# Two attentions and an expert layer on one core: the prologue's projections over several PSUM banks, its transfers and rows in another order, and the second batch's causal attention split around the first batch's eight-wide queries

## The chip, the cores and the metric

The kernel runs on one NeuronCore of a Trainium2 chip. The metric is the device time of one execution in microseconds (us); lower is better. A core has TensorE (PE, matrix multiplies into PSUM), VectorE (DVE), ScalarE (ACT), GpSimd (POOL) and SyncE (SP, which here only issues transfers). Each engine runs its own instruction list in order; they meet at semaphores. PSUM has eight banks, and each is named in this kernel: scores0 to scores2, max0 to max2, out and side.

## The reference, cut to what matters

There are eight batches of 512 tokens by 256 features. Each goes through a modulated layer norm, a causal attention with 16 heads of width 16, a gate and a residual; then a second modulated layer norm, a third norm with an affine, an attention without mask with 32 heads of width 8 (here called the eight-wide attention), and experts with a gelu.

```
mod = (_silu(L0_c) @ L0_wmod).reshape(L0_c.shape[0], 6, 1, -1)
h = _layernorm(x, axis=-1) * (1 + ca) + sa
x = x + ga * _L0_attn_ref(h, q_proj, k_proj, v_proj, o_proj)       # 16 heads of width 16, causal
h = _layernorm(x, axis=-1) * (1 + cb) + sb
    xn = (x - mu) / jnp.sqrt(var + 1e-05) * ln_g + ln_b
    att = jnp.einsum('bqhd,bkhd->bhqk', q, k) / np.float32(np.sqrt(hd))   # 32 heads of width 8
    o = jnp.einsum('bhqk,bkhd->bqhd', p, v).reshape(B, S, D) @ wo + x
    h = jax.nn.gelu(jnp.einsum('metd,edf->metf', xe, w1) + b1[None, :, None, :], approximate=False)
    y = jnp.einsum('metf,efd->metd', h, w2) + b2[None, :, None, :]
x = x + gb * _L0_ffn_ref(h, ...)
```

## The kernel before

**Pieces.** The work is a list of items, such as `("scores", off, a, s, k)` or `("qk", off, a, t, oc, half)`, where `off` is the batch (counted from the section's first), `a` is 0 for the causal attention and 1 for the eight-wide one. Every engine walks the same list (`walk`) and executes its own share of each item. So the order of the list is the order on every engine, SP's transfers included. The sections are `start`, `first` and `second` (the prologue for batch 0), `before` (the rest of batch 0 and 1 that comes ahead of the loop), `loop` (six turns, written for batches 0 and up) and `after`.

**One projection.** A `qk` item is four fp32 matmul records on PE into one bank (L1085), a bf16 copy of the top part on ACT (L913), the rest on DVE (L1364), which frees the bank, and two further bf16 parts on POOL (L776, L778). After every second item SP stores three parts to HBM with three transfers (L693). The parts of a whole projection are read back by `stacks` items (L626), which load the operand stacks `q_stack` and `k_stack` of one unit of eight heads. All of it goes through the bank `side`, one item at a time. `to_features` is a transpose by PE into a bank (L1062) with an affine out of it (DVE L1350 or ACT L934); `v` is a projection (L1095) that ACT copies out (L920).

**One attention.** A step `s` is four heads times 128 rows. `maxima` computes its products (L1118) and DVE reduces them (L1375 with mask, L1378 without); after four steps `max_rows` turns the maxima (L1127), POOL splits them in bf16 parts, and SP writes them with three small transfers into `q_stack` (L712). `scores` (L1147) may start on a group of four steps only when those transfers have landed. ACT exponentiates (L949), POOL masks (L812), `values` multiplies by v (L1164), `sums_out` copies out, `normalise` turns (L1173) and divides. `attention(main, lead, beside, ...)` weaves the `scores` of the steps in `main` with the `maxima` of later steps in `lead`; `beside` hangs other items at numbered slots, four to a position.

**The eight-wide queries of batch 0.** In `before`, main is the 16 steps of batch 0's causal attention and then the 16 of batch 1's. Batch 0's output projection, both norms (`layernorm` items with n = 1 and n = 2; pieces 0 to 2 take moments, 3 to 5 a first guess on DVE, 6 is a chain of small POOL steps, 7 and 8 the scaling), the features and the eight-wide projections hang beside the steps of batch 1. When the stacks of unit 2 have landed, the `maxima` of the eight-wide attention begin, and eight steps of them stand ahead of the loop.

**The prologue.** SP loads x and four weights, then writes 18 constant transfers. PE turns two weights, makes the modulation columns, and makes batch 0's features and eight projections. Then ACT waits for the stored parts and issues the loads of unit 0's keys, PE makes v, then the modulation rows, and DVE works out the gates. PE waits for all of it before the first `maxima`.

## Time and profile before

| | us |
|---|---|
| median of 3 runs | 1787.32 |
| lowest and highest | 1782.77, 1788.34 |
| profiled execution, its own time | 1787.78 |
| span of the profiled execution | 1786.0 |
| mean granted TensorE clock | 0.965 |

The profile is one execution: every instruction with its start and duration, which semaphore released it, and the transfers. PE is busy for 1513.0 us of the span (85%), DVE for 1154.7 (65%), ACT for 1006.8 (56%) and POOL for 532.8 (30%). A steady turn of the loop takes about 201 us. What is changed lies ahead of the loop, in the first 258 us, where PE waits more than it does later.

### The profile page before, as it was taken

The page shows a single profiled execution, that of the slowest core. Times are in us where ns is not written, and L with a number is a line of the kernel's source. Part 1 is how long each engine was busy: PE and PEld are TensorE (multiplying, and loading weights), DVE is VectorE, ACT ScalarE, POOL GpSimd, SP SyncE. Part 2 cuts the span into 40 slices and gives each one's busy share as a digit, 9 for nine tenths or more (in the row PEclk, how much of TensorE's full clock was granted, in tenths as well). Part 3 has the DMA queues.
Part 4 walks back from the last instruction along what each step waited for, and adds up shares of the span by engine and source line. Part 5 has one row for each costly group of instructions (what it writes and reads, how often), then busy time and mean ns, then how long its engine had stood idle before and what let it go on. Part 6 is the DMA issues. An engine that isn't in the chain of part 4 may idle for free.

```text
span 1786.0 us, 30231 instructions
## 1 busy us (share of the span) xinstructions
PE 1513.0 (85%) x10001; PEld 663.9 (37%) x10001; DVE 1154.7 (65%) x2961; ACT 1006.8 (56%) x2095; POOL 532.8 (30%) x1245
## 2 busy tenths in 40 slices
PE   5578759998899888998899889998899887879767
PEld 4223313335333443335333443335333442314315
DVE  3456459864797559864797559864797557775430
ACT  1044426764577546764577546764577545666571
POOL 3133414331342224331342224331342224300100
PEclk9689859999999999999999999999999998999999
DMA  7542242352344233352334233352334223212301
GB/s 224 122 113 64 74 128 69 88 135 75 107 121 101 81 98 109 95 135 75 107 117 105 81 101 101 100 134 75 104 117 108 81 71 85 72 43 63 95 1 59
DMA packets 137542, 171.26 MB, mean 96 GB/s; under 512 B 17000, under 2 KB 103080, under 8 KB 137392
## 3 DMA queue, kind: packets, MB, share of 16 engines
q1 hardware_dynamic: 132336, 165.88, 33.8%
q10 hardware_dynamic: 5056, 3.45, 0.7%
q8 instruction: 86, 1.41, 0.3%
q14 instruction: 64, 0.52, 0.1%
HBM read 110.67 MB, written 56.66 MB: 94 GB/s over the span
## 4 chain that ended last, share of the span: by engine, by line
PE 64%; DVE 17%; ACT 8%; issue 5%; DMA 3%; POOL 1%; SPq 1%; ACTq 0%; POOLq 0%; DVEq 0%
PE bank_out L1164 15%; PE bank_scores L1147 10%; DVE neg_max L1378 8%; PE bank_max L1118 7%; PE bank_side L1085 7%; PE bank_side L1251 7%; ACT probs L949 4%; PE bank_side L1095 4%; PE bank_side L1235 3%; PE bank_scores L1235 3%; PE bank_side L1173 2%; PE bank_side L1216 2%; DVE normed L1337 2%; PE bank_side L1207 2%; DMA q_stack<-max_parts 2%
## 5 line engine op out<-in xcount | busy, mean ns | idle before, releaser
L949 ACT ACTIVATE probs<-bank_scores 128x512 f32<-128x512 f32 (+3 forms) x1536 | 753.1, 544 | 424.7 <-PE bank_scores L1147 415.6
L1378 DVE TENSOR_REDUCE neg_max<-bank_max 128x1 f32<-128x512 f32 x1024 | 654.2, 684 | 185.4 <-PE bank_max L1118 180.5
L1147 PE MATMUL bank_scores<-q_stack,k_stack 64*128 64x512 bf16 (+3 forms) x2048 | 319.1, 348 | 94.7 <-ACT probs L949 67.7
L1164 PE MATMUL bank_out<-probs,v_tile 128*9 128x512 f32 (+4 forms) x3072 | 368.7, 552 | 19.3 <-ACT out_raw L963 12.3
L1118 PE MATMUL bank_max<-k_stack,q_stack 64*128 64x512 bf16 (+3 forms) x2048 | 321.6, 350 | 70.4 <-DVE neg_max L1378 41.6
L1375 DVE CUSTOM_DVE_ANT_0 bank_max<-bank_max,causal 128x384 f32<-128x384 f32 (+3 forms) x512 | 241.8, 515 | 100.7 <-PE bank_max L1118 98.1
L1147 PEld LDWEIGHTS bank_scores<-q_stack,k_stack 64*128 64x128 bf16 x2048 | 85.0, 94 | 369.4 <-issue 334.9
L812 POOL TENSOR_SCALAR_AFFINE_SELECT probs<-probs 128x512 f32<-128x512 f32 x128 | 81.0, 633 | 357.7 <-ACT probs L949 357.7
L1118 PEld LDWEIGHTS bank_max<-k_stack,q_stack 64*128 64x128 bf16 x2048 | 105.8, 95 | 159.5 <-issue 104.8
L794 POOL CAST max_parts<-max_row 16x128 bf16<-16x128 f32 x96 | 28.7, 298 | 373.4 <-DVE max_row L1389 373.4
L1251 PE MATMUL bank_side<-w_out,hidden_T 128*128 128x256 f32 x512 | 118.8, 385 | 4.8 <-issue 2.7
L1251 PEld LDWEIGHTS bank_side<-w_out,hidden_T 128*128 128x128 f32 x512 | 94.6, 190 | 35.0 <-DVE max_row L1389 11.1
L1164 PEld LDWEIGHTS bank_out<-probs,v_tile 128*9 128x9 f32 (+1 forms) x3072 | 47.5, 91 | 137.5 <-issue 82.4
L1424 DVE TENSOR_TENSOR y_out<-bank_side,gb_bc 128x256 f32<-128x256 f32 x32 | 13.6, 425 | 122.9 <-PE bank_side L1251 122.9
L1085 PE MATMUL bank_side<-act_T,wq 128*128 128x256 f32 x256 | 79.0, 434 | 12.9 <-DVE act_T L1350 5.2
L1095 PE MATMUL bank_side<-wv,act_T 128*128 128x256 f32 x256 | 75.2, 418 | 13.6 <-ACT v_tile L920 8.1
L1085 PE MATMUL bank_side<-act_T,wk 128*128 128x256 f32 x256 | 76.1, 422 | 10.2 <-DVE rest L1364 5.8
L776 POOL CAST partsq<-rest 128x256 bf16<-128x256 f32 x64 | 25.4, 396 | 169.7 <-DVE rest L1364 169.6
L1375 DVE DVE_READ_ACCUMULATOR2_ANT neg_max<- 128x1 f32 x512 | 72.8, 142 | 0.0
L913 ACT ACTIVATE partsq<-bank_side 128x256 bf16<-128x256 f32 x64 | 24.7, 386 | 79.0 <-PE bank_side L1085 79.0
L1173 PE MATMUL bank_side<-ident,out_raw 128*128 128x128 f32 x384 | 63.0, 287 | 7.1 <-DVE rest L1364 4.2
L1173 PEld LDWEIGHTS bank_side<-ident,out_raw 128*128 128x128 f32 x384 | 40.8, 142 | 74.3 <-issue 72.7
(120 smaller groups left out, 1555.0 us busy)
## 6 DMA issues: line engine op xcount, KB each, us to landing
q_stack<-q_parts SPq DMA_DIRECT2D x128, 256.0 KB, 4.3
k_stack<-k_parts SPq DMA_DIRECT2D x124, 192.0 KB, 6.0
w_in<-in_L_ffn_w_dram SPq DMA_DIRECT2D x16, 1024.0 KB, 5.9
w_out<-in_L_ffn_w_dram SPq DMA_DIRECT2D x16, 1024.0 KB, 8.4
q_parts<-partsq SPq DMA_DIRECT2D x32, 384.0 KB, 2.6
k_parts<-partsk SPq DMA_DIRECT2D x32, 384.0 KB, 2.6
q_parts<-partsq SPq DMA_DIRECT2D x32, 256.0 KB, 2.9
k_parts<-partsk SPq DMA_DIRECT2D x32, 256.0 KB, 2.9
```

The lines of the kernel that those rows point to most:

```text
L812: pool.affine_select(out=tile, in_=tile, compare_op=ALU.is_ge, fill=0.0, base=0, pattern=[[0, GROUP], [1, P]], channel_multiplier=-1).then ...
L949: nc.scalar.activation(probs[s % 2][:, head_at(k), q0:S], region[bank][:, q0:S], ACT.Exp, scale=float(WIDTH[a]) ** -0.5).then_inc(drained[ ...
L1085: ins = pe.matmul(region[bank][:, 0:S // 2], w_qkv[a][t][:, cc, oc * P:(oc + 1) * P], act_T[:, cc, cols], start=(cc == 0), stop=(cc == C - 1))
L1095: ins = pe.matmul(region[bank][:, 0:D], act_T[:, cc, t * P:(t + 1) * P], w_qkv[a][2][:, cc, :], start=(cc == 0), stop=(cc == C - 1))
L1118: ins = pe.matmul(region[to][:, 0:keys], q_stack[buf][rows, at, qt * P:(qt + 1) * P], k_stack[buf][rows, at, 0:keys], start=(i == 0), stop ...
L1147: ins = pe.matmul(region[to][:, q0:S], k_stack[buf][rows, at, kt * P:(kt + 1) * P], q_stack[buf][rows, at, q0:S], start=(i == 0), stop=last)
L1164: ins = pe.matmul(outb[32 * k:32 * k + WIDTH[a] + 1, q0:S], v_tile[a][:, kt, g * GROUP + k, :], probs[s % 2][:, k, q0:S], start=(kt == 0), ...
L1173: ins = pe.transpose(side[:, t * P:(t + 1) * P], out_raw[:, g % 2, t * P:(t + 1) * P], ident[:, :])
L1235: ins = pe.matmul(region[bank][:, k * EXP_TOK:(k + 1) * EXP_TOK], w_in[:, cc, ft * P:(ft + 1) * P], expert_xT[:, cc, j * EXP_TOK:(j + 1) * ...
L1251: ins = pe.matmul(region[bank][:, 0:D], hidden_T[:, ft, k * P:(k + 1) * P], w_out[:, ft, :], start=(ft == 0), stop=(ft == FT - 1))
L1375: v.tensor_tensor_reduce(region[bank][:, 0:keys], region[bank][:, 0:keys], causal[:, S - keys:S], 1.0, -3e38, ALU.add, ALU.max, dst).then_ ...
L1378: v.tensor_reduce(dst, region[bank], AX_X, ALU.max).then_inc(drained[bank], 1)
```

## The change

- `first` and `second`: the two features, the eight projections and the four v of batch 0 take the banks side, scores0 and scores2 in turn. The scaling of batch 0's norm stands ahead of the modulation columns on DVE (section `scale`). The loads of wv1 and wo1 move from SP to ACT. The modulation rows come ahead of v on PE, and the gates ahead of the eight-wide weights' reordering on DVE. `stacks 0 0` comes after v.
- `before`: v of batch 1 is made at slots 23 to 35 into `v_next` and copied to its place by the new item `first_v` at slot 67. `stacks 1 0` moves from slot 18 to 25. The norm pieces stand closer together. `main` is cut at three quarters: after eight steps of batch 1 all that waits is flushed, then come the norm's scaling, the features and the eight eight-wide projections with nothing between, over the banks side, max0, max1 and max2; then `stacks 0 2`, whose keys ACT loads; and the last eight steps with v and the maxima beside them.

```diff
-    first = [*norm[NEWTON_PIECE + 1:], ("load_x", 1), *features_items(0, 0)]
+    scale = [*norm[NEWTON_PIECE + 1:]]
+    first = [("load_x", 1), *features_items(0, 0)]
     for n, item in enumerate(qk_0):
         first.append(item)
-        if n == 7:
-            first.append(("stacks", 0, 0))
         first += norm_1[n - 3:n - 2] if 3 <= n < 7 else norm_1[4:NEWTON_PIECE + 1] if n == 7 else []
-    second = v_items(0, 0)
+    second = [*v_items(0, 0), ("stacks", 0, 0)]
...
     place_at(beside, (1, 7, 9, 13, 17), qk_items(0, 1)[3:])
-    place(beside, 18, [("stacks", 1, 0)])
+    place_at(beside, (23, 27, 31, 35), v_items(0, 1))
+    place(beside, 25, [("stacks", 1, 0)])
     place(beside, 38, [("stacks", 1, 1)])
-    place_at(beside, (67, 67, 69, 69), v_items(0, 1))
+    place(beside, 67, [("first_v", 1)])
     place_at(beside, (72, 72), [("head_features", 0, 0, 0), ("head_features", 0, 0, 1)])
-    place_at(beside, (75, 75, 77, 77), out_items(0))
+    norm_1, norm_2 = layernorm_items(0, 1), layernorm_items(0, 2)
+    place_at(beside, (75, 75, 77), out_items(0)[:3])
+    place(beside, 77, [norm_1[0], out_items(0)[3]], 0)
+    place(beside, 79, norm_1[1:NEWTON_PIECE + 1], 0)
     place(beside, 82, [("load_residual", 1), ("load_gate", 0)])
-    place_norm(beside, (77, 79, 79, 80, 80, 80, 80, 85, 86), 0, 1)
-    place_norm(beside, (87, 88, 88, 89, 89, 89, 89, 93, 94), 0, 2)
+    place(beside, 83, norm_1[NEWTON_PIECE + 1:] + norm_2[:NEWTON_PIECE + 1], 0)
     place(beside, 91, [("load_mod", 1)])
-    place_at(beside, (95, 97), features_items(0, 2))
-    place_at(beside, (99, 101, 103, 105, 107, 109, 111, 113), qk_items(1, 0))
-    place(beside, 113, [("stacks", 0, 2)])
-    place_at(beside, (115, 117, 118, 119), v_items(1, 0))
-    place_at(beside, (121, 123), features_items(0, 1))
...
+    half = 3 * len(main) // 4
+    left = []
+    before += attention(main[:half], ahead[FIRST_LEAD:], beside, early, left, rows_after=(1, ROWS_AFTER),
+                        sooner={("normalise", 0, 0, 3): (17, 3)})
+    before += [item for kind in ("values", "sums_out", "max_rows", "normalise") for at, item in left if item[0] == kind]
+    before += norm_2[NEWTON_PIECE + 1:] + features_items(0, 2) + qk_items(1, 0) + [("stacks", 0, 2)]
+    beside = {}
+    place_at(beside, (1, 3, 5, 7), v_items(1, 0))
+    place_at(beside, (9, 11), features_items(0, 1))
+    place(beside, 14, [("keep_v", 0), ("keep_x", 0)])
+    place(beside, 13, [("stacks", 0, 3)])
     first_2 = steps_of_attention(0, 1)[:LEAD]
...
+    lead = [(), (), tuple(first_2[0:2]), tuple(first_2[2:4]), *one_each(first_2[4:])]
+    before += attention(main[half:], lead, beside, hand_on=handed)
...
+EARLY_NAMES = ("first", "second", "before")
+EARLY_BANKS = dict(zip(features_items(0, 0) + qk_items(0, 0) + v_items(0, 0), itertools.cycle(("side", "scores0", "scores2"))))
+EARLY_BANKS.update(zip(features_items(0, 2) + qk_items(1, 0), itertools.cycle(("side", "max0", "max1", "max2"))))
...
-                if b or u:
+                if b or u not in (0, 2):
                     load_stack(sp, b, u, k_dram, k_stack, products)
...
-            for i, w in enumerate((wq1, wk1, wv1, wo1)):
+            for i, w in enumerate((wq1, wk1)):
...
+            act.dma_start(stage_w[2], wv1.rearrange("(c p) n -> p c n", p=P)).then_inc(weights_in, 16)
...
+            act.dma_start(stage_w[3], wo1.rearrange("(c p) n -> p c n", p=P)).then_inc(weights_in, 16)
...
+            def first_v(b, f):
+
+                wait(act, values_done[0], steps_of[0] * b)
+                wait(act, drained["side"], number(last_v[0]) + 1)
+                nc.scalar.activation(v_tile[0][:, :, :, 0:WIDTH[0]], next_values(0), ACT.Copy).then_inc(first_v_kept, 1)
...
+                    if a == 0 and b == 1 and s == 0:
+                        pe.wait_ge(first_v_kept, 1)
```

On PE in the prologue, from the modulation columns to the first maxima, the list before is this (names are bank <- operands; x2 is two matmuls):

```order
L1044 MATMUL bank_scores<-silu,probs 128x8 x8
L1062 MATMUL bank_side<-ident,normed 128x128 x8
L1085 MATMUL bank_side<-act_T,wq 128x256 x8
L1085 MATMUL bank_side<-act_T,wk 128x256 x8
L1033 MATMUL bank_max<-ident,w_in 128x128 x4
L1033 MATMUL bank_scores<-ident,w_in 128x128 x4
L1262 MATMUL bank_scores<-ident,w_out 128x64
L1095 MATMUL bank_side<-wv,act_T 128x256 x8
L1271 MATMUL bank_max<-probs,silu 8x256 x2
L1271 MATMUL bank_max<-probs,silu 8x512 x2
L1271 MATMUL bank_scores<-probs,silu 8x256 x2
L1118 MATMUL bank_max<-k_stack,q_stack 128x128 x8
```

And now, from the last of the projections:

```order
L1117 MATMUL bank_side<-act_T,wk 128x256 x2
L1063 MATMUL bank_out<-ident,w_in 128x128 x4
L1063 MATMUL bank_max<-ident,w_in 128x128 x4
L1296 MATMUL bank_scores<-ident,w_out 128x64
L1303 MATMUL bank_max<-probs,silu 8x512 x2
L1303 MATMUL bank_max<-probs,silu 8x256 x4
L1308 MATMUL bank_out<-zeros 128x128 x4
L1127 MATMUL bank_scores<-wv,act_T 128x256 x4
L1127 MATMUL bank_side<-wv,act_T 128x256 x2
L1127 MATMUL bank_scores<-wv,act_T 128x256 x2
L1150 MATMUL bank_max<-k_stack,q_stack 128x128 x8
```

The rows of the modulation (8x256 and 8x512) now stand ahead of v, and the projections and v write more banks than one.

On SP, where batch 1's first stacks and batch 0's third group of maxima are stored and loaded, before:

```order
L693 DMA k_parts<-partsk 128x512
L626 DMA q_stack<-q_parts 64x2x1024 x4
L626 DMA k_stack<-k_parts 48x2x1024 x4
L712 DMA q_stack<-max_parts 2x8x128 x6
L626 DMA q_stack<-q_parts 64x2x1024 x4
```

And now:

```order
L711 DMA k_parts<-partsk 128x512
L730 DMA q_stack<-max_parts 2x8x128 x3
L640 DMA q_stack<-q_parts 64x2x1024 x4
L640 DMA k_stack<-k_parts 48x2x1024 x4
L730 DMA q_stack<-max_parts 2x8x128 x3
L640 DMA q_stack<-q_parts 64x2x1024 x4
```

Three of the six small transfers now stand ahead of the eight loads of unit 0.

On ACT, around the eight-wide projections, now (L937 is the top part of a projection, L976 the exponential, L947 the copy of v):

```order
L961 ACTIVATE act_T<-bank_max,lnb_T,lng_T 128x512
L937 ACTIVATE partsq<-bank_max 128x256 x2
L937 ACTIVATE partsq<-bank_side 128x256
L937 ACTIVATE partsq<-bank_max 128x256
L937 ACTIVATE partsk<-bank_max 128x256 x2
L937 ACTIVATE partsk<-bank_side 128x256
L937 ACTIVATE partsk<-bank_max 128x256
L640 DMA k_stack<-k_parts 48x2x1024 x2
L976 ACTIVATE probs<-bank_scores 128x512 x2
L947 ACTIVATE v_next<-bank_side 128x256
L976 ACTIVATE probs<-bank_scores 128x512 x2
```

Before, exponentials stood between the top parts, and no transfer of ACT was here: two key loads, which wait for the stored parts, now stand ahead of the exponentials of batch 1's ninth step.

## Rows read from the trace of the kernel before

**Rows 1.** The page: span of the profiled execution.
```profile
span 1786.0 us, 30231 instructions
```
**Rows 2.** Stretches: busy us of each engine (instructions), granted clock, DMA share, GB/s.
```profile
117.30:127.30 10.00, 0.02 (x2) 0.02 (x4) 0.60 (x4) 0.00 (x0) 0.00 (x0) 0.65 0.89 177
...
173.20:231.20 58.00, 39.50 (x272) 16.52 (x272) 25.60 (x91) 23.86 (x59) 23.78 (x62) 0.87 0.32 99
231.20:257.90 26.70, 16.05 (x73) 5.28 (x75) 20.00 (x33) 4.35 (x10) 2.66 (x6) 0.50 0.17 47
257.90:1786.00 1528.10, 1339.30 (x8925) 585.19 (x8921) 1026.68 (x2526) 934.39 (x1914) 456.47 (x1060) 0.99 0.34 93
```
**Rows 3.** Timeline of the prologue: start us, us, engine, line, what [idle before].
```profile
13.91 1.38 DVE L1337 TENSOR_SCALAR normed<-x_in,mean_var,rstd 128x256 f32<-128x256 f32 x4
...
15.35 1.12 PE L1062 MATMUL bank_side<-ident,normed 128*128 128x128 f32 x4 [1.76 <-DVE normed L1337]
...
19.39 2.08 PE L1085 MATMUL bank_side<-act_T,wq 128*128 128x256 f32 x4 [0.90 <-DVE act_T L1350]
...
40.44 2.07 PE L1085 MATMUL bank_side<-act_T,wk 128*128 128x256 f32 x4 [0.93 <-DVE rest L1364]
...
43.16 1.06 PE L1033 MATMUL bank_scores<-ident,w_in 128*128 128x128 f32 x4
...
43.45 0.40 POOL L776 CAST partsk<-rest 128x256 bf16<-128x256 f32 x1 [1.86 <-DVE rest L1364]
...
43.93 0.67 POOL L778 TENSOR_TENSOR partsk<-rest,partsk 128x256 bf16<-128x256 f32 x1
...
44.59 1.38 PE L1095 MATMUL bank_side<-wv,act_T 128*128 128x256 f32 x4
...
48.30 2.05 ACTq L626 DMA_DIRECT2D k_stack<-k_parts  x4
...
59.07 2.75 PE L1271 MATMUL bank_max<-probs,silu 128*8 128x256 f32 x8
...
66.90 0.40 PE L1118 MATMUL bank_max<-k_stack,q_stack 64*128 64x128 bf16 x4 [4.21 <-issue]
```
**Rows 4.** The two loads of x_in, issued at 1.0 and 16.2: issue to landing.
```profile
DMA to landing us min/median/max: 4.5/8.6/12.6
```
**Rows 5.** Stack loads of L626: unit 0 (issued 48.3 to 50.3), unit 1 (67.2 to 71.4).
```profile
DMA to landing us min/median/max: 3.3/6.9/9.4
...
DMA to landing us min/median/max: 3.8/5.9/7.8
```
**Rows 6.** Timeline at batch 0's third group of steps.
```profile
115.52 2.58 SPq L626 DMA_DIRECT2D q_stack<-q_parts  x4
...
120.33 16.40 SPq L712 DMA_DIRECT2D q_stack<-max_parts  x6
...
127.28 1.03 PE L1147 MATMUL bank_scores<-q_stack,k_stack 64*128 64x512 bf16 x4 [9.99 <-DMA q_stack<-max_parts]
```
**Rows 7.** Batch 1's first v on PE (timeline), and the copies of v by keep_v.
```profile
152.94 1.13 PE L1095 MATMUL bank_side<-wv,act_T 128*128 128x256 f32 x4
...
L1000 ACT ACTIVATE v_tile<-v_next x2: 1053/1062/1071, 242.1 to 387.0; 128x1024 f32<-128x1024 f32 x2
```
**Rows 8.** Timeline of the second and third norm of batch 0.
```profile
176.69 0.17 DVE L1296 TENSOR_SCALAR rstd<-root 128x4 int32<-128x4 int32 x1
...
180.65 1.25 DVE L1302 SCALAR_TENSOR_TENSOR normed<-x,mean_var,mod_bc 128x256 f32<-128x256 f32 x2 [1.83 <-POOL rstd L871]
...
195.69 1.09 PE L1062 MATMUL bank_side<-ident,normed 128*128 128x128 f32 x4 [1.36 <-DVE normed L1337]
```
**Rows 9.** Timeline: unit 2's stacks are loaded, and the eight-wide maxima begin.
```profile
224.65 1.29 SPq L626 DMA_DIRECT2D q_stack<-q_parts  x2
...
231.17 0.61 PE L1118 MATMUL bank_max<-k_stack,q_stack 64*128 64x512 bf16 x2 [4.26 <-DMA k_stack<-k_parts]
```
**Rows 10.** Groups of instructions from 231 to 258.2, costliest: busy us, mean ns | idle before.
```profile
L1378 DVE TENSOR_REDUCE neg_max<-bank_max 128x1 f32<-128x512 f32 x31 | 20.0, 687 | 18.3 <-PE bank_max L1118 18.3
```

More of the change, by code:

```diff
@@ L247, in sections @@
     place_at(beside, (18, 22, 26), qk_items(0, 1)[:3])
[L248 to L249 removed]
+    main = steps_of_attention(0, 0) + steps_of_attention(1, 0)
+    ahead = one_each(main)
+    early, handed = [], []
     before += attention([], ahead[:FIRST_LEAD], beside, hand_on=early, sooner={("max_rows", 0, 0, 0): (4, 1)})
@@ L263, in sections @@
-    place_at(beside, (99, 101, 103, 105, 107, 109, 111, 113), qk_items(1, 0))
-    place(beside, 113, [("stacks", 0, 2)])
-    place_at(beside, (115, 117, 118, 119), v_items(1, 0))
-    place_at(beside, (121, 123), features_items(0, 1))
-    place(beside, 124, [("keep_v", 0), ("keep_x", 0)])
-    place(beside, 126, [("stacks", 0, 3)])
-    first_2 = steps_of_attention(0, 1)[:LEAD]
-    ahead = ahead[FIRST_LEAD:]
-    ahead += [()] * (30 - len(ahead)) + [tuple(first_2[0:2]), tuple(first_2[2:4])]
@@ L272, in sections @@
-    handed = []
-    before += attention(steps_of_attention(0, 0) + steps_of_attention(1, 0), ahead, beside, early, handed,
-                        rows_after=(1, ROWS_AFTER), sooner={("normalise", 0, 0, 3): (17, 3), ("max_rows", 0, 1, 0): None})
-    before += attention([], [tuple(first_2[4:6]), tuple(first_2[6:8])], {1: [("max_rows", 0, 1, 0)]}, hand_on=handed)
+    half = 3 * len(main) // 4
+    left = []
+    before += attention(main[:half], ahead[FIRST_LEAD:], beside, early, left, rows_after=(1, ROWS_AFTER),
+                        sooner={("normalise", 0, 0, 3): (17, 3)})
@@ L333, in sections, with banks_of @@
     after = [item for item in after if item != ("keep_x", 2)]
-    return (("start", start), ("first", first), ("second", second), ("before", before), ("loop", loop), ("after", after))
-def banks_of(item):
+    return (("start", start), ("scale", scale), ("first", first), ("second", second), ("before", before), ("loop", loop), ("after", after))
+EARLY_NAMES = ("first", "second", "before")
+EARLY_BANKS = dict(zip(features_items(0, 0) + qk_items(0, 0) + v_items(0, 0), itertools.cycle(("side", "scores0", "scores2"))))
+EARLY_BANKS.update(zip(features_items(0, 2) + qk_items(1, 0), itertools.cycle(("side", "max0", "max1", "max2"))))
+def banks_of(item, name):
     kind = item[0]
@@ L370, in number_fills @@
             fills[name, item] = []
-            for bank in banks_of(item):
+            for bank in banks_of(item, name):
                 assert bank not in unfinished, (name, item)
@@ L738, in _ @@
                       .then_inc(ones_in, 16)
-            walk(sp, {"load_x": load_x, "qk": qk, "stacks": stacks}, ("first",))
+            walk(sp, {"load_x": load_x, "qk": qk, "stacks": stacks}, ("first", "second"))
             sp.wait_ge(mod_rows_made, 4)
@@ L1025, in _ @@
             pe.wait_ge(const_made, 7)
-            for k in range(4):
-                pe.matmul(outb[:, k * P:(k + 1) * P], zeros[:, :], zeros[:, :], start=True, stop=True)
             def turn_weight(i, bank):
@@ L1082, in qk @@
                 start_fill(f[0])
+                if b == 0 and a == 1:
+                    wait(pe, perm_done, 4)
                 cols = slice(half * (S // 2), (half + 1) * (S // 2))
```

83 lines of the change are left out of this document (48 added, 35 removed).

## The prediction

> **What bounds the kernel now.** I read the page for the span and then cut the trace into stretches. From 257.9 us on, where the loop begins, the granted clock is 0.99 and PE is busy 88% of the time [rows 2]; the code there does not change. So a gain is made ahead of the loop and is handed on undiminished: the question is only when the loop's first scores start, now at 257.9. I then went through the timeline for the waits of PE ahead of it. There are four.
>
> First, the prologue: the first maxima start at 66.90 [rows 3]. The eight projections run from 19.39 to 42.5, one each 3.0 us, though PE works 2.07 us on each: with one bank, the next waits until ACT and DVE have emptied it [rows 3]. Their last part is split by POOL at 44.60, the stored parts have landed at 48.30, and only then do the loads of unit 0 go out [rows 3]. PE meanwhile makes v late, because ACT waits for those parts before it copies the first v. The modulation rows begin at 59.07, and from there matmuls and gates take 7.8 us to the first maxima [rows 3].
>
> Second, 9.99 us in which nothing computes: the scores of batch 0's third group wait for small transfers, issued at 120.33 behind eight stack loads that began at 115.52 [rows 6, 2]. Third, the two norms: PE has little to do, while POOL's chain keeps DVE from the first guess at 176.86 to 180.65, and the same again in the next norm, until the features at 195.69 [rows 8]. Fourth, the wait of 4.26 us for unit 2's stacks, and behind it 26.7 us in which DVE reduces 31 maxima for 20.0 us, PE is busy 16.05 us and the clock is at 0.50, the lower of its two levels, 1.2 GHz [rows 2, 9, 10].
>
> **The change part by part.** I sum against the profiled execution, 1787.78 us with a span of 1786.0 [rows 1]; it lies 0.46 above the median of the runs, which is nothing here.
>
> *(a) The prologue.* The scalings no longer wait for the modulation columns, so the transposes start about when the scalings start now, 13.9 instead of 15.35, and the second transpose goes to another bank without waiting 0.9 for the first to be emptied: the projections start at 17.0 instead of 19.39 [rows 3]. With three banks PE goes back to back: eight by 2.07 ends at 33.6. At the higher level (about 1.1 each, by the v rows [rows 7]) it would end sooner, but not to much use: batch 1's x lands at 16.2 + 12.6 = 28.8 [rows 4], and its moments stand on DVE between the fourth and fifth rest, so four rests and four POOL pairs of 0.40 and 0.67 come after that, 34 to 35 either way. Moving wv1 and wo1 to ACT changes no bytes, so I leave 28.8. Last split now 2.1 after the last matmul [rows 3]: 35.0. Stores 3.7 (48.30 less 44.60) gives 38.7, against 48.30.
> Unit 0's eight loads took 11.4 us from 48.30: the first landed after 3.3, the others one each 1.17, and unit 1's eight took as long from one queue as these from two [rows 5]. The four query loads go out at 38.7 and are in at 45.5. The key loads wait on ACT for four v. PE: turned weights 2 us, modulation rows 3.6 (of the 7.8), then v. In the row at 44.59 the four records of v took 1.38 and the rows of a warm PE are 1.13 [rows 3, 7]; that is 4.5 to 8.3 for four, so the key loads go out at 43.5 to 48. SP sends unit 1's loads from about 43, once the gates are done, and they share the engines with the keys: eight loads by 1.17 from 45.5 end at 54.9. First maxima at 55.5 instead of 66.90: **−11.4**. Ends: −14 (keys served first), −8 (keys out at 48 and last, 59). The reordered weights on DVE (four copies) cost nothing: DVE idles until the maxima; without that cover they would cost about 1 us.
> That two queues share is also what the Trainium skill says (DMA: Bandwidth & Descriptors, section Issuing engines are not separate DMA queues).
> The skill's page TensorE: Matmul & The Clock Gate (section Part 4: PE-mode transpose) says that transposes do not count as PE being busy and so do not bring the higher level. Here the rows differ: after the turned weights at 43.16, which are transposes, v at 44.59 already ran between the levels [rows 3]. By the page v would take 8.3 us and the sum would be 3 us worse; by the row it takes about 5.
>
> *(b) The stall at 117.3.* The small transfers now stand ahead of the stack loads on SP, so they leave when POOL has split them, before 115.52, and land before PE asks for them. The 9.99 us go [rows 6]. Four v of batch 1 now stand here, 1.13 each, 4.5 [rows 7]. What is late next is batch 1's own unit 0: its eight loads start at 115.52 as before and need 12, so they are in at 127.4 [rows 5, 6], and PE would reach batch 1's first maxima at 117.3 + 4.5 + about 3.5 = 125.3. PE waits 2.1 there. Now those maxima come some 5.1 after 127.28, at 132.4. Gain: 132.4 − 127.4 = **−5.0**, with the v already paid. Ends −5.5 and −3.
>
> *(c) v out of the later place.* Four v leave (4.5 and their waits for the side bank, 5.6 in all). `first_v` copies 1024 elements a partition, like keep_v's 1.06 us [rows 7], on ACT between batch 0's last values and batch 1's first; the exponentials of the next step are queued behind it and `values` waits for both. PE has 2 us of work to cover that; about 2 us are left over: **−3.5**. Ends −4.5, −2.
>
> *(d) The norms and the split.* The DVE guess of the second norm comes 1.1 earlier (two maxima no longer stand ahead of it), the scaling and the third norm's moments are contiguous, 1.6 more: its guess is ready 2.6 earlier. But its POOL chain (3.9, the gap from 176.86 to 180.65 [rows 8]) now has three steps of attention and the last maxima in front of the scaling, and the flush: I get the features at 201 instead of 195.69, 5.5 later. The eight projections are then bare: POOL's 0.40 + 0.67 with gaps, 1.2 each [rows 3], sets their pace, 9.6, plus 2 to the last split, 3.7 to the stores: loads out at 219 against 224.65 [rows 9]. ACT waits for those parts before it issues the two key loads (1 us), with the exponentials of step 9 queued behind it, so PE stands still until about 220; then four v and the rest of two and a half steps take 7. The loads are in by 224.5; the eight-wide maxima start at 227 instead of 231.17. From there DVE needs 32 reductions by 0.687 = 22 [rows 10], with a gap to each pair 23.4, and with turns 24.5; the scores and values of six steps lie in PE's free time. Loop at 251.5 to 252 instead of 257.9: **−6**. Ends: −10 (no still stand of ACT, PE's higher level in the norms), +2 (PE and DVE wait on each other, 8 us).
>
> *(e) The loop's start.* PE now enters it at 0.50 [rows 2]. With scores and values among the maxima it is likelier to be at the higher level: **−1** (ends −2, 0).
>
> Sum: 11.4 + 5.0 + 3.5 + 6 + 1 = 26.9; 1787.8 − 26.9 = **1761**.
>
> **The rivals.** *Keys last (0.10).* v runs at 2.07 each, the keys go out at 48 behind unit 1's queue and unit 0 completes last, at 59 to 60. Then (a) is −7.5: 1765. For it: PE is at the lower level until 42 [rows 3]. Its time is inside my range.
> *The bare block costs what it gives (0.10).* Eight steps of scores that used to fill the gaps between projections now come after them. If the flush is long and ACT's wait blocks four v and three steps, (d) becomes +5: 1772.
> *Not what it says (0.03).* Unit 0 of batch 1 lands later still, since the keys of batch 0 and its own loads meet, and the prologue stays bound by unit 0's loads at 62: (a) −5, (b) 0, (c) −2, (d) +2: about 1783, no change to measure. Against it: the two queue orders are plain in the list.
> *Slower (0.05).* One mechanism: in the last eight steps scores, values and eight-wide maxima do not overlap but take turns. PE at the lower level needs some 3.6 us a position (1.2 for maxima, 0.9 for scores, 1 for values, the rest for turns) and DVE 2.9 [rows 10]; one after the other that is 6.5 by 8 = 52 instead of 24.5, (d) is +22 and the kernel stands at 1789; with ACT's exponentials in the row too (0.9 a position), 1796. It decides from 6.7 us a position on. Against it: three max banks and three scores banks, so PE can work on one while DVE reads another.
> *More (0.06).* Keys first, PE warm in the first maxima, (d) at −10: 1748 or less.
> My forecast, 1752 to 1770, has the remaining 0.66.
>
> **How the numbers follow.** The forecast's range and the two rivals near it give 1750 to 1776, with 0.86; the rest is 0.06 below and 0.08 above. A measurement of this kernel can tell about 0.3%, 5.4 us, from no change. Faster: 0.66 + 0.10 + 0.10 + 0.06 = 0.92; same 0.03; slower 0.05.
>
> **What would show it.** (a) First maxima near 55.5, projections one each 2.1 or less, and the wait before the maxima ended by a stack load. (b) No wait of scores on the small transfers; a short one of maxima on batch 1's stack. (c) The copy of v_next beside batch 0's last values. (d) Features some 5 us later against batch 0's last v, loads of unit 2 some 5 us earlier; the maxima of the eight-wide attention at 1.5 us a pair among scores. The loop's first scores at 231, then steady turns as before. I am wrong if those pairs take 2 us and more, if the first maxima stand after 60, or if the loop's first turn is longer than now.

## The result, and the profile after

| | before | after |
|---|---|---|
| median, lowest and highest of 4 runs each, us | 1785.8 (1782.77 to 1788.34) | 1758.8 (1755.25 to 1759.74) |
| profiled execution and its span, us | 1787.78, 1786.0 | 1755.25, 1753.5 |
| mean granted TensorE clock | 0.965 | 0.970 |

The ratio after to before is 0.9846, 95% interval 0.9824 to 0.9868: 27.5 us less (3.9 either way). 1761 was predicted, with 1750 to 1776 as the range.

The profiled execution of after is the fastest of its four. From 457.6 us on, where the code is that of before, to the end of the last batch it took 1293.3 us; before took 1297.3 for the same part. So 4 us of its lead are no part of the change.

**After, prologue.** Timeline; columns as in [rows 3]. The projections are L1117 here, v L1127, the maxima L1150, stack loads L640.

```profile
16.36 2.08 PE L1117 MATMUL bank_scores<-act_T,wq 128*128 128x256 f32 x4 [0.90 <-DVE act_T L1385]
...
21.66 1.03 PE L1117 MATMUL bank_side<-act_T,wk 128*128 128x256 f32 x4
...
28.98 0.75 DVE L1354 BATCH_NORM_STATS2 stats<-x_in 128x6 f32<-128x256 f32 x2 [6.27 <-DMA x_in<-_L_attn_in_features_dram]
29.65 0.41 DVE L1399 TENSOR_TENSOR rest<-bank_side,partsk 128x256 f32<-128x256 f32 x1
...
30.11 2.07 PE L1117 MATMUL bank_side<-act_T,wk 128*128 128x256 f32 x4 [5.70 <-DVE rest L1399]
...
31.98 1.06 PE L1063 MATMUL bank_out<-ident,w_in 128*128 128x128 f32 x4
...
33.87 0.67 POOL L796 TENSOR_TENSOR partsk<-rest,partsk 128x256 bf16<-128x256 f32 x1
...
39.49 1.03 PE L1127 MATMUL bank_side<-wv,act_T 128*128 128x256 f32 x4
...
39.80 2.61 SPq L640 DMA_DIRECT2D q_stack<-q_parts  x4
...
41.49 2.16 ACTq L640 DMA_DIRECT2D k_stack<-k_parts  x4
```

The projections start at 16.36 instead of 19.39, and seven of the eight run back to back, from the third on at the higher level (granted clock 1.0 from 19.9 to 26.8). In the fifth row the last one waits 5.70: DVE stood 6.27 in front of batch 1's x, with the `rest` that would free PE's bank queued behind it. Last split 34.5, loads out at 39.8 and 41.5. The waits of PE up to 60 us (engine, what, releaser; total, times, longest) put a stack load ahead of the first maxima:

```profile
PE bank_max L1150 <- DMA k_stack<-k_parts: 10.3, 1, 10.3
...
PE bank_side L1117 <- DVE rest L1399: 5.7, 1, 5.7
```

The first maxima start at 51.64, instead of 66.90 [rows 3].

**After, batch 0's third group and batch 1's first maxima.** Timeline.

```profile
103.49 2.00 SPq L640 DMA_DIRECT2D k_stack<-k_parts  x4
...
104.22 1.13 PE L1127 MATMUL bank_side<-wv,act_T 128*128 128x256 f32 x4
...
105.28 0.61 PE L1179 MATMUL bank_scores<-q_stack,k_stack 64*128 64x512 bf16 x4
...
112.33 0.40 PE L1150 MATMUL bank_max<-k_stack,q_stack 64*128 64x128 bf16 x4 [2.63 <-DMA k_stack<-k_parts]
```

The scores of the third group (105.28) wait for nothing; before, they waited 9.99 [rows 6]. Instead 2.63 stand in front of batch 1's maxima. Behind batch 0's last values (134.31) comes the new copy on ACT; PE's waits from 131 to 140 add up to under 2 us, and none is over 0.4:

```profile
134.37 1.06 ACT L1028 ACTIVATE v_tile<-v_next 128x1024 f32<-128x1024 f32 x1
```

**After, the bare block.** Timeline, from the features on.

```profile
178.08 1.09 PE L1092 MATMUL bank_side<-ident,normed 128*128 128x128 f32 x4 [2.19 <-DVE normed L1372]
...
180.89 3.40 PE L1117 MATMUL bank_max<-act_T,wq 128*128 128x256 f32 x8 [0.87 <-ACT act_T L961]
...
184.12 1.03 PE L1117 MATMUL bank_side<-act_T,wq 128*128 128x256 f32 x4
...
188.44 1.03 PE L1117 MATMUL bank_max<-act_T,wk 128*128 128x256 f32 x4
...
192.24 0.67 POOL L796 TENSOR_TENSOR partsk<-rest,partsk 128x256 bf16<-128x256 f32 x1
197.19 2.61 SPq L640 DMA_DIRECT2D q_stack<-q_parts  x4
197.19 0.82 ACTq L640 DMA_DIRECT2D k_stack<-k_parts  x2
198.11 1.08 ACT L976 ACTIVATE probs<-bank_scores 128x512 f32<-128x512 f32 x2 [8.23 <-DMA k_parts<-partsk]
...
198.85 1.04 PE L1179 MATMUL bank_scores<-q_stack,k_stack 64*128 64x512 bf16 x4 [7.79 <-ACT probs L976]
```

The eight projections take 8.6 us, at the higher level from the third on (the granted clock rises at 183.8). Then ACT waits for the stored parts with the exponentials of step 9 queued behind it, and PE waits 7.79 us for those, as the prediction had it. The loop's first scores start at 231.1.

**After, stretches.** Columns as in [rows 2]: the norms and the bare block, the eight steps with the eight-wide maxima, and the rest.

```profile
149.90:207.50 57.60, 34.80 (x208) 17.84 (x204) 24.60 (x88) 17.27 (x41) 20.58 (x57) 0.76 0.39 110
207.50:230.70 23.20, 16.97 (x133) 5.87 (x135) 19.64 (x34) 11.49 (x29) 5.15 (x10) 0.85 0.04 7
230.70:1753.50 1522.80, 1336.63 (x8931) 584.76 (x8923) 1025.70 (x2525) 934.29 (x1914) 456.75 (x1060) 0.99 0.33 93
```

Against [rows 2] and [rows 10]: the 26.7 us in which DVE worked 20.0 are now 23.2 with 19.6 of DVE, but PE's 133 matmul records (73 before) lie in them, and the clock is 0.85, not 0.50.

### The profile page after: what moved, and what is told of

Its sections match the earlier page's. It is cut to its first block, busy times and chain, and to the rows that moved or that the text cites. A ratio compares the mean times of both kernels' runs of the same rounds, so it can differ in the third digit from the quotient of the medians.

```text
span 1753.5 us, 30245 instructions
## 1 busy us (share of the span) xinstructions
PE 1495.6 (85%) x10001; PEld 662.1 (38%) x10001; DVE 1153.1 (66%) x2961; ACT 1007.8 (57%) x2096; POOL 531.6 (30%) x1245
## 4 chain that ended last, share of the span: by engine, by line
PE 64%; DVE 16%; ACT 8%; issue 5%; DMA 3%; POOL 2%; SPq 1%; ACTq 0%; POOLq 0%; DVEq 0%
PE bank_out L1198 16%; PE bank_scores L1179 10%; DVE neg_max L1413 8%; PE bank_max L1150 7%; PE bank_side L1285 7%; PE bank_side L1117 5%; ACT probs L976 5%; PE bank_side L1127 4%; PE bank_side L1269 3%; PE bank_scores L1269 3%; PE bank_side L1207 2%; PE bank_side L1241 2%; PE bank_side L1250 2%; DVE normed L1372 2%; DMA k_stack<-k_parts 1%
## 5 line engine op out<-in xcount | busy, mean ns | idle before, releaser
L976 ACT ACTIVATE probs<-bank_scores 128x512 f32<-128x512 f32 (+3 forms) x1536 | 753.2, 544 | 411.5 <-PE bank_scores L1179 394.2
L1150 PE MATMUL bank_max<-k_stack,q_stack 64*128 64x512 bf16 (+3 forms) x2048 | 316.7, 345 | 73.6 <-DVE neg_max L1413 36.9
L1150 PEld LDWEIGHTS bank_max<-k_stack,q_stack 64*128 64x128 bf16 x2048 | 105.6, 95 | 157.5 <-issue 108.6
L1459 DVE TENSOR_TENSOR y_out<-bank_side,gb_bc 128x256 f32<-128x256 f32 x32 | 13.6, 425 | 122.9 <-PE bank_side L1285 122.9
L1117 PE MATMUL bank_side<-act_T,wk 128*128 128x256 f32 x236 | 67.4, 409 | 10.8 <-DVE rest L1399 6.5
L1117 PE MATMUL bank_side<-act_T,wq 128*128 128x256 f32 x232 | 69.0, 422 | 8.0 <-DVE act_T L1385 4.3
L1127 PE MATMUL bank_side<-wv,act_T 128*128 128x256 f32 x244 | 70.6, 413 | 4.3 <-ACT act_T L961 2.0
L1269 PE MATMUL bank_side<-expert_xT,w_in 128*128 128x256 f32 x256 | 63.5, 391 | 1.5 <-DVE expert_xT L1452 0.9
```

The lines of the kernel that those rows point to most:

```text
L976: nc.scalar.activation(probs[s % 2][:, head_at(k), q0:S], region[bank][:, q0:S], ACT.Exp, scale=float(WIDTH[a]) ** -0.5).then_inc(drained[ ...
L1117: ins = pe.matmul(region[bank][:, 0:S // 2], w_qkv[a][t][:, cc, oc * P:(oc + 1) * P], act_T[:, cc, cols], start=(cc == 0), stop=(cc == C - 1))
L1127: ins = pe.matmul(region[bank][:, 0:D], act_T[:, cc, t * P:(t + 1) * P], w_qkv[a][2][:, cc, :], start=(cc == 0), stop=(cc == C - 1))
L1150: ins = pe.matmul(region[to][:, 0:keys], q_stack[buf][rows, at, qt * P:(qt + 1) * P], k_stack[buf][rows, at, 0:keys], start=(i == 0), stop ...
L1269: ins = pe.matmul(region[bank][:, k * EXP_TOK:(k + 1) * EXP_TOK], w_in[:, cc, ft * P:(ft + 1) * P], expert_xT[:, cc, j * EXP_TOK:(j + 1) * ...
```

## The experiments

Line numbers shift a little between kernels. Where a position is compared, it is the time from the span's start at which the trace's semaphores show the work done. Each kernel ran beside before on the same chip, whose median then was 1785.66 (e1 to e4), 1786.71 (e5 to e8) and 1787.25 (e9, e10); the gain is one less the ratio, times 1786. A batch's x is here the one after its causal attention. Batch 1's x is ready shortly after the loop has begun, and from batch 1's x to batch 2's is one whole turn of the loop.

| kernel | first maxima | batch 0's last values | last of 32 eight-wide maxima | median us | ratio (95%) | gain |
|---|---|---|---|---|---|---|
| before | 67.28 | 153.06 | 258.17 | 1785.8 | 1 | 0 |
| e1 banks only | 53.42 | 140.48 | 246.21 | 1773.24 | 0.9924 (0.9905, 0.9942) | 13.6 |
| e2 prologue only | 54.18 | 140.75 | 246.14 | 1771.53 | 0.9907 (0.9886, 0.9929) | 16.6 |
| e3 stacks later | 66.76 | 147.52 | 252.73 | 1781.47 | 0.9970 (0.9959, 0.9981) | 5.4 |
| e4 no split | 54.55 | 136.75 | 238.15 | 1767.81 | 0.9887 (0.9868, 0.9906) | 20.2 |
| after | 52.02 | 134.31 | 230.65 | 1758.8 | 0.9846 (0.9824, 0.9868) | 27.5 |
| e9 split, one bank | 52.35 | 134.91 | 245.05 | 1772.34 | 0.9916 (0.9895, 0.9937) | 15.0 |
| e10 quarter maxima | 52.38 | 135.31 | 226.37 | 1751.49 | 0.9796 (0.9774, 0.9817) | 36.4 |

### e1: the kernel before, with only the banks of the prologue in turn

```diff
+EARLY_BANKS = dict(zip(features_items(0, 0) + qk_items(0, 0) + v_items(0, 0), itertools.cycle(("side", "scores0", "scores2"))))
...
-            turn_weight(3, region["scores0"])
+            turn_weight(3, outb)
```
(The turned b1 goes to max2, since scores2 is in use.)

> The kernel before with one part of the change alone: batch 0's two features, eight projections and four v take the banks side, scores0 and scores2 in turn (the turned output weight and the bias move to other banks for it); order of transfers, of rows and of the scalings stays. My theory: the one bank set the pace of 3.0 us a projection. With three banks PE makes them at 2.1 or less until DVE stands still for batch 1's x (29 us), the last POOL split is at about 35.5 instead of 44.6, unit 0's loads go out at 39.5 instead of 48.3, and as v, rows and gates still follow one another behind ACT's wait, the first maxima start at about 55 instead of 66.9 (51.6 in the changed kernel): 1774 us against 1785.8. Rival: the order of rows and transfers carries the prologue's gain and the banks little, as POOL's 1.1 us a projection and the wait for x keep the last split late: first maxima at 62 or later, 1781.

Measured 1773.24, as the theory had it, with the first maxima at 53.42 (their start at 53.13, 55 said). The banks alone bring 13.6 us. What ends last is no longer the stacks, which are in at 51.5, but the modulation rows and the gates made from them; timeline:

```profile
44.12 3.93 PE L1278 MATMUL bank_max<-probs,silu 128*8 128x256 f32 x8
...
48.95 0.41 DVE L1471 TENSOR_SCALAR hidden_T<-bank_max 8x256 f32<-8x256 f32 x1 [13.26 <-PE bank_scores L1278]
...
53.13 0.29 PE L1124 MATMUL bank_max<-k_stack,q_stack 64*128 64x128 bf16 x4 [4.21 <-DVE hidden_T L1483]
```

### e2: the whole new prologue, everything behind it as before

```diff
-    place_at(beside, (23, 27, 31, 35), v_items(0, 1))
-    place(beside, 25, [("stacks", 1, 0)])
+    place(beside, 18, [("stacks", 1, 0)])
...
-EARLY_BANKS.update(zip(features_items(0, 2) + qk_items(1, 0), itertools.cycle(("side", "max0", "max1", "max2"))))
```
(and the slots from 67 on, the split and unit 2's keys as in before)

> The changed kernel with its prologue alone (banks in turn, scalings first, wv1 and wo1 loaded by ACT, modulation rows ahead of v, keys after v); everything behind the first maxima as before. My theory: the parts add up, so the first maxima start at 51.6 as in the changed kernel, the 10 us stall of batch 0's third group comes back, and the time is 15.3 us under that of before: 1770.5. Rival: the later parts need one another, and the earlier start is in part lost again before the loop (the stack loads meet other transfers): 1775 or more, with the loop's first scores less than 13 us earlier than at 257.9.

Measured 1771.53. The intervals of e1 and e2 overlap: that the other orders in the prologue (scalings first, rows before v, transfers on ACT, keys after v) give anything beyond the banks is not shown. Those orders take away only one of two things, stacks and rows, that end within 2 us of each other.

The first maxima start at 53.80, and not at 51.64 as in after, though the prologue is the same code:

```profile
34.36 4.46 PE L1296 MATMUL bank_max<-probs,silu 128*8 128x512 f32 x12
...
42.76 1.94 ACTq L635 DMA_DIRECT2D k_stack<-k_parts  x4
...
53.80 0.40 PE L1145 MATMUL bank_max<-k_stack,q_stack 64*128 64x128 bf16 x4 [11.14 <-DMA k_stack<-k_parts]
```

Six kernels share this prologue, and they fall into two groups by the moment at which the granted clock comes back to 1.0. In after, e9 and e10 it comes back at 33.6 to 34.5: the modulation rows take 3.6 to 3.9 us, the keys go out from 41.5 to 41.8 on, and the first maxima are done at 52.0 to 52.4. In e2, e4 and e6 it comes back at 35.9 to 36.1: the rows take 4.5, the keys go out from 42.5 to 42.8 on, two of the four behind the first load of unit 1 on SP (43.1 to 43.4) where it is one in after, and the first maxima are done at 54.2 to 54.6. So some 2 us in the prologue belong to the execution rather than to the code. Why the clock comes back at the one moment or the other is not shown.

### e3: the kernel before, with batch 1's first stack loads seven slots later

```diff
-    place(beside, 18, [("stacks", 1, 0)])
+    place(beside, 25, [("stacks", 1, 0)])
```

> The kernel before with one number changed: batch 1's stacks of unit 0 at slot 25 instead of 18, so that three small transfers stand ahead of their loads on SP; v of batch 1 stays at its late place. My theory: the wait of 9.99 us of the scores goes, but the eight loads are in at 127.4 as before and PE now comes to batch 1's first maxima at about 121, 4.5 us sooner than with the four v there, and waits some 6 us for them: the maxima start at 127.4 to 128 instead of 132.4, the clock falls in the wait, and 3.5 to 5 us are gained: 1781.5. The v as filler are then worth nothing at this place by themselves. Rival: the four v made this gain; without them the wait for small transfers only changes its name, and the time stays at 1785 to 1787.

Measured 1781.47, as the theory had it. The stall of 9.99 is gone, and the waits of PE from 100 to 135 show what is late next. The four v are not there to fill this wait, so it is longer than after's 2.63:

```profile
PE bank_max L1118 <- DMA k_stack<-k_parts: 7.3, 1, 7.3
```

### e4: the changed kernel without the split

```diff
-    before += norm_2[NEWTON_PIECE + 1:] + features_items(0, 2) + qk_items(1, 0) + [("stacks", 0, 2)]
...
+    place_at(beside, (95, 97), features_items(0, 2))
+    place_at(beside, (99, 101, 103, 105, 107, 109, 111, 113), qk_items(1, 0))
+    place(beside, 113, [("stacks", 0, 2)])
```
(all of `before` from slot 72 on as in the kernel before, and unit 2's keys on SP again; the copy of v and the later slot of batch 1's stack loads as changed)

> The changed kernel with the eight-wide part undone: norms, features, projections and loads of batch 0's eight-wide attention woven between the steps of batch 1 on the bank side, as before; prologue, stacks and v of batch 1 as changed. My theory: values of batch 1's third step end at 149.7 as in the changed kernel, the eight-wide maxima begin at 208 (they begin at 207.5 in the changed one), and the loop's first scores come at 234.5 instead of 230.7: the split is worth 4 us, 1762.5. Rival: the split gains nothing, because the bare block costs what the fuller end gives: 1758.5, within 1.5 us of the changed kernel. Second rival: it is worth more, 8 us and over, since without it the last maxima stand alone at the lower clock: 1767.

Measured 1767.81. The theory's 4 us for the split was too little: it is worth 7.3 us by the ratios and 9.0 by the medians, near the second rival. The stretch of the eight-wide maxima is that of [rows 2] again, the same 26.7 us at 0.50:

```profile
211.50:238.20 26.70, 16.05 (x75) 5.21 (x73) 20.16 (x34) 4.35 (x10) 2.67 (x6) 0.50 0.18 48
```

Counted from batch 0's x (152.35 here, 149.90 in after), the features are ready after 23.4 us here and 29.3 in after, unit 2's parts are stored after 52.0 and 47.3, and the last of the 32 maxima come after 85.8 and 80.75. So 5.05 are won ahead of the loop. Without the split this last figure varies from run to run: it is 84.7 in before and 84.8 to 85.4 in e1 to e3, so against before the split wins 4.0. Another 2.2 are won from there to batch 1's x. From that to batch 2's, one whole turn, this kernel took 205.2 us, after's 202.4 and before's 201.3, at granted clocks of 0.98, 0.99 and 1.00. Whether e4's longer turn is its own or chance is open.

### e5 to e8: what the changed kernel could still give

e5: batch 1's first moments after all eight projections, so that no `rest` waits behind x.

```diff
-        first += norm_1[n - 3:n - 2] if 3 <= n < 7 else norm_1[4:NEWTON_PIECE + 1] if n == 7 else []
+        first += norm_1[0:NEWTON_PIECE + 1] if n == 7 else []
```

> The changed kernel with one thing moved: the moments of batch 1's first norm, which wait on DVE for batch 1's x (landed at 29.0), stand behind batch 0's eight projections instead of among them. My theory: that wait holds DVE's rest of the fifth projection, and through it the last split (34.6), the stored parts and unit 0's loads, which end the wait before the first maxima. Without it the last split is at about 28.5, the parts are stored at 33, unit 0 is in at 46, and the first maxima start at 46.5 instead of 51.6 to 54: 5 to 7 us, 1753. Rival: the transfers are the bound and not DVE, since the queue is full until x lands at 29 and the parts stand behind it: parts stored at 37 and more, and less than 3 us gained, 1756.5.

Measured 1755.96 (0.9837, 0.9817 to 0.9857): not told from after, as the rival said. The last split is done at 28.7 instead of 34.5, but the parts are stored at 37.5 instead of 39.8, and the first maxima fill at 50.3 instead of 52.0. Six us on the engines become two in the stores. Its stretches say why; the DMA share and the rate stand at the rows' ends:

```profile
28.00:37.50 9.50, 5.78 (x29) 3.76 (x27) 8.41 (x31) 1.53 (x4) 3.35 (x14) 1.00 0.97 339
37.50:50.00 12.50, 0.12 (x4) 0.15 (x4) 0.10 (x1) 0.00 (x0) 0.00 (x0) 0.61 0.98 175
```

The 16 transfer engines are full all the time: when the first stores are sent (22.2), constants and x are still arriving, until 28.9, and behind the stores the stacks follow.

e6: SP loads the keys of unit 2 again, so that ACT does not wait for parts in the eight-wide block. The expectation also speaks of unit 0, but this edit leaves unit 0's keys on ACT, as they are in the kernel before.

```diff
-                if b or u not in (0, 2):
+                if b or u:
```

> The changed kernel with one thing undone: the keys of units 0 and 2 of batch 0 are loaded by SP behind the queries, as all others, and not by ACT. My theory: in the eight-wide part ACT no longer stands 8.2 us for the stored parts with the exponentials of batch 1's ninth step behind it, so PE fills that wait with v and two steps, the eight-wide maxima begin when unit 2's loads are in, at 204.5 instead of 207.5, and the last of them ends 2.5 to 3.5 us sooner; in the prologue the keys go out behind four queries from one queue and come in by 51.5 as before, since the two queues share the same rate: 1755.5. Rival: DVE's maxima are the bound from 204 on and two issued key loads come 1 us later, so nothing is gained: 1758 to 1760.

Measured 1756.18 (0.9848, 0.9821 to 0.9874): not told from after. The trace still has unit 0's keys on ACT:

```profile
42.48 1.93 ACTq L640 DMA_DIRECT2D k_stack<-k_parts  x4
```

In the block, ACT's wait and the 7.8 us of PE behind it are gone. The waits of PE from 192 to 211 show what took their place:

```profile
PE bank_max L1150 <- DMA k_stack<-k_parts: 7.9, 1, 7.9
```

Counted from batch 0's x, the eight-wide maxima begin 2.0 us sooner than in after, but the last come only 0.3 sooner: the stretch takes 24.9 us at a clock of 0.68, against 23.2 at 0.85.

```profile
207.90:232.80 24.90, 18.70 (x133) 6.42 (x135) 19.86 (x34) 10.97 (x27) 5.15 (x10) 0.68 0.12 25
```

e7: both edits (here too, unit 0's keys stay on ACT).

> The changed kernel with both edits, moments late and all keys on SP. My theory: the two lie in different stretches and add up, 8 to 9 us: 1750. Rival: the prologue's part and that of the eight-wide block share a bound (SP's queue, which now issues all loads), so that the pair gains no more than the better one: 1753 to 1755.

Measured 1757.06 (0.9839, 0.9818 to 0.9860). The two do not add up, and 1750 was wrong. The rival's shared bound is not shown either: neither edit alone can be told from after.

e8: the keys of unit 0 ahead of v again.

```diff
-    second = [*v_items(0, 0), ("stacks", 0, 0)]
+    second = [("stacks", 0, 0), *v_items(0, 0)]
```

> The changed kernel with one thing undone: ACT issues unit 0's keys ahead of the copies of v, as before, so that they go out with the queries at 39.8 instead of 41.5 to 42.8, ahead of unit 1's loads. My theory: the 16 loads share one rate of 1.1 to 1.2 us each, and the keys behind v meet few of unit 1's; unit 0 is in at 51 to 51.5 against 51.5 to 54 and the first maxima start 0 to 2 us sooner, while v, now behind ACT's wait for the parts, ends at about 46 and holds nobody: 1757.5. Rival: v behind the wait brings PE's clock down and v to 48 and later, and its order was a gain: no change or 1 to 3 us slower.

Measured 1759.07 (0.9847, 0.9826 to 0.9869), and first maxima at 52.17 where after has 52.02. The keys go out at 39.99 instead of 41.49, and it gives nothing: the maxima now wait for the queries (timeline), while the transfer engines have a share of 0.97 from 40 to 51.8 us. This is the rival's "no change".

```profile
51.79 0.40 PE L1150 MATMUL bank_max<-k_stack,q_stack 64*128 64x128 bf16 x4 [6.30 <-DMA q_stack<-q_parts]
```

### e9: the split kept, but its features and projections in one bank

```diff
-EARLY_BANKS.update(zip(features_items(0, 2) + qk_items(1, 0), itertools.cycle(("side", "max0", "max1", "max2"))))
```

> The changed kernel, with the third norm's features and the eight eight-wide projections of batch 0 again all in the bank side, and everything else as changed. Theory: with one bank a projection has to wait for ACT (0.39) and DVE (0.42) and two handovers before the next, so about 2.2 us instead of the 1.2 measured between their starts; eight take about 8 us longer. Part of it comes back, since the 12 stores then do not queue up behind each other (about 1 us). Nothing else stands beside this block, so the stored parts, the eight-wide maxima and the loop all come 7 us later: 1766. Rival, the stores set the end of the block whatever the projections do (3 MB at 340 GB/s are 9 us), and the eight steps behind have slack: 3 us or less, 1759 to 1762.

Measured 1772.34: 12.5 us slower than after by the ratios, nearly twice the 7 that I expected, and its gain of 15.0 is no better than the 20.2 of e4, which has no split at all (their intervals just overlap; at the last of the 32 maxima e9 is 6.9 us behind e4). The timeline shows each projection at the lower level, with the gap for ACT and DVE in front of it:

```profile
197.68 2.08 PE L1116 MATMUL bank_side<-act_T,wk 128*128 128x256 f32 x4 [0.93 <-DVE rest L1398]
```

Eight of them fill 23.2 us. This is the stretch in e9, and then that of after:

```profile
182.60:205.80 23.20, 16.63 (x34) 9.50 (x36) 2.97 (x7) 2.69 (x7) 7.47 (x14) 0.50 0.31 103
```
```profile
180.80:189.60 8.80, 8.71 (x34) 7.11 (x36) 2.97 (x7) 2.83 (x9) 5.12 (x11) 0.83 0.27 90
```

The same 34 records are 16.6 us of PE in the one and 8.7 in the other: 7.9 us for the clock. What PE idles is 6.6 against 0.1: 6.5 us for the gaps. My expectation had the gaps and left the clock where after has it; the clock was the larger half. Where the parts are stored the loss is 14.4 us (211.54 against 197.17).

### e10: the first 32 eight-wide maxima over a quarter of the keys

```diff
-                    v.tensor_reduce(dst, region[bank], AX_X, ALU.max).then_inc(drained[bank], 1)
+                    v.tensor_reduce(dst, region[bank][:, 0:S // 4] if b == 0 and s < 8 else region[bank], AX_X, ALU.max).then_inc(drained[bank], 1)
```

> The changed kernel, but the first 32 eight-wide maxima of batch 0 (the 32 ahead of the loop) are taken over a quarter of the keys only: the work left out is three quarters of those 32 reductions on DVE, about 0.5 us each, 16 us of DVE in all; PE makes the same products. Theory: DVE sets the pace from the first eight-wide maxima to the loop (20 of 23.5 us busy), so without it PE's own work is the bound there, 17.3 us of matmuls and some handovers: 3.5 to 4.5 us gained, 1754.5. Rival, DVE and PE take turns and the handovers set the pace: more, 8 us and over, 1751 or less. Third, PE or ACT sets it already and DVE waits: under 1.5 us, 1758.

Measured 1751.49, 8.9 us less than after by the ratios, give or take some 5. In the profiled run the stretch itself (from the first to the last of the 32) takes 17.3 us against 23.1, 5.8 less:

```profile
209.10:226.40 17.30, 13.66 (x131) 5.21 (x135) 8.13 (x34) 11.29 (x29) 4.54 (x9) 1.00 0.02 4
```

DVE did 11.5 us less, and half of it shows. The stretch lies between the theory (3.5 to 4.5) and its rival (8 and over): DVE is what PE waits for there, and when it is lighter PE's work is the next bound (13.7 of 17.3). PE's own busy time fell by 3.3 without a matmul less, because the clock went from 0.85 to 1.00. So the 5.8 are no pure price of DVE. The 3 us by which the medians say more lie within their noise.

## Why the prediction was right, step by step

The total was right (1758.8 for 1761). The terms are read where each stage ends. The profiled run of after leads that of before by 15.3 us at the first maxima, 18.75 at batch 0's last values, 23.5 at batch 0's x, 27.5 at the last of the 32 maxima, 29.7 at batch 1's x and 28.5 at batch 2's; the medians differ by 27.0. About 2.3 of it is chance in the prologue: e2 and e4 have the same prologue as after and reach the first maxima 13.1 and 12.7 us earlier than before, after itself 15.3, since its clock came back earlier (see e2). The terms missed in both directions, so part of the close agreement is luck.

- **(a) the prologue, −11.4 said, −12.7 to −15.3 measured.** The order of events was right: the wait on batch 1's x (28.8 said, 28.98), last split (35.0; 34.5), parts stored (38.7; 39.8), a stack load as the last releaser. The mis-sized term is the start of the key loads: 43.5 to 48 said, 41.5 measured. My terms bring PE to v at 39.2 (33.6 and the 2 and 3.6 in front of v), and I gave the four v 4.5 to 8.3. PE came to v at 37.71, because the eight projections were done at 32.0 and not at 33.6, and the four v took 3.7, because the modulation rows in front of them had run at the higher level since 33.6. So unit 0 was in at 51.6, not 54.9. A slip besides: 33.6 and 2.1 make a last split at 35.7, not 35.0. That the higher level would be of little use to the projections was right, though not for the one reason that I gave, batch 1's x: e5 takes x out of the way, and the full transfer engines then leave 2 of its 6 us.
- **What brings (a).** I gave the change's many edits one sum. e1 shows that the banks alone give nearly all of it.
- **(b) the stall, −5.0 said, −3.5 to −4.4 measured.** From the first maxima to batch 0's last values, with the four v among them, the stage is 4.4 shorter in e4 than in e2, and 3.5 shorter in after than in before. Without the v it is 5.0 shorter (e3, whose median is 1781.47 for 1785.66). The remaining wait is 2.63 for 2.1 said.
- **(c) v moved, −3.5 said, −4.8 measured** (the gain grows from 18.75 to 23.5 between batch 0's last values and batch 0's x, and from 4.0 to 8.8 from e2 to e4). I left about 2 us over for the copy on ACT; the waits of PE there show only fractions of one.
- **(d) the split, −6 said, −4.0 measured against before and −5.05 against e4, up to the loop.** Counted from batch 0's x, the features come 5.9 later (5.5 said), and the loads go out 3.9 earlier than in before and 4.8 earlier than in e4 (5.6 said). ACT and PE stood still as said, 8.23 and 7.79. From the features (201) to the loads (219) I had 18, of which my terms name 15.3; 19.1 were measured, and the 2.8 of the features themselves are what the terms leave out. The projections took 8.6 for the 9.6 said, but the last split came 3.4 behind them, not 2, since POOL runs 1.07 a piece behind a faster PE, and the stores took 4.3, not 3.7. The maxima began 10.0 behind the loads' issue instead of 8, and took 23.1 (1.44 a pair) instead of 24.5.
- **(e) the loop's start, −1 said, −2.2 measured** at batch 1's x in the profiled runs (from the last of the 32 maxima: 26.7 before and in e4, 24.5 after). By batch 2's x 1.1 of it is given back, so −1.0 is left. The sign that I named, a longer first turn, did not come: from the last of the 32 maxima to the same event one turn later it is 203.5 in before and 202.4 in after. By the medians of e4 and after, (d) and (e) are 9.0 together for 7 said; the interval does not exclude either.

Of the rivals, *Keys last* did not come: v ran at 1.03, not 2.07, and the keys went out at 41.5, not 48; e8 sends them earlier still and nothing moves. *The bare block costs what it gives* is what e9 shows when the block has one bank. I had tied it to a long flush and ACT's wait, and e6 shows that ACT's wait alone is worth next to nothing; the banks and the clock decide it. *Slower* needed 6.7 us a position; it was 23.1 / 8 = 2.9. *More* was put at 1748 or less, but even the best ends of all my terms (14, 5.5, 4.5, 10 and 2) give only 1752, and what a warm PE would add had no price.

On the clock, one page of the Trainium skill was weighed in the prediction (TensorE: Matmul & The Clock Gate, section Part 4: PE-mode transpose: transposes do not count as PE being busy). The four v took 3.7 us here (37.71 to 41.39), not the 8.3 that followed from it. The granted clock is 0.5 from 26.8 and 1.0 from 33.6, which falls into the last of eight transposes (31.98 to 33.80); but a projection stands in front of them, so this trace alone does not refute it.

## What to carry to other kernels

When a chain of fp32 matmuls shares one PSUM bank, price the gap and also the clock: with a gap of 0.93 the level stayed at 0.50 and each took 2.07 (e9), without it six of the eight took 1.03 (after), so a projection went from 3.0 us to little over 1. Moving such work out of the shade of an attention and into a bare block paid only with several banks; with one (e9) it gained no more than leaving it in the shade (e4), and in the profiled runs it was behind. Before making the engines in front of a transfer faster, look at the DMA share there: at 0.97 six us of engine time were worth two (e5).

## What the runs showed of the hardware that I had not expected

- The clock of after was at the lower level from 43.8 us until 78.0, through PE's wait for the stacks and the first maxima, and again at 0.5 in the norms (156.5 to 166.7, 176.9 to 183.8) and through the wait for the stores and behind it (194.0 to 204.2), yet 1.0 from 183.8 to 194.0, through most of the bare block; e9, whose PE is 16.6 of 23.2 us busy there, had 0.50 throughout.
- The moment at which the level comes back differs by 2.5 us between executions of the same prologue (33.6 in after, 36.1 in e2), and with it go 2.2 us at the first maxima.
- The stores and loads of the prologue reach 339 GB/s with a share of 0.97, but the stack loads and the small transfers beside them only 175 GB/s with a share of 0.98 (e5).
- The last part of the kernel, from batch 2's x on, is the same code in all twelve kernels but took 1290.7 (e5) to 1297.9 us (e1) in the profiled runs, with a granted clock of 0.988 to 0.995 over it (0.995 in the two shortest, e5 and e6). So two single runs cannot tell a difference under some 7 us, and e5, e6 and e7, each with at least one wait less than after, cannot be ranked against it.
